# Who sends the finished blocks of the recurrence: SyncE's queue or GpSimd's own

## The chip, the cores and the metric

The kernel runs on one core of a Trainium2 chip. A core has five engines with an instruction stream each: TensorE (PE), VectorE (DVE), ScalarE (ACT), GpSimd (POOL) and SyncE (SP), which here does nothing but issue transfers and wait on semaphores. Transfers (DMAs) run on the core's 16 DMA engines, whichever engine issued them. The metric is the device time of one execution in microseconds (us). The kernel before takes 1922.44 us, the median of three runs (1921.51 to 1926.3).

## The reference, cut to what matters

The input is `x` (2, 64, 256, 256) in float32. There are two layers:

- `x = x + depthwise_conv3x3(ln_c(x))`
- `t = t + rnn(ln_t(t))`, with the 65536 pixels of a batch as a sequence. `Wx = x @ W.T` is normalised over batch and sequence (gamma, beta), and then a scan runs over the sequence: `y = sigmoid(wx_t + y @ V.T)`. The result is called x2 here (x1 is what the convolution left).
- `x = x + linear_attention(ln_c(x))`
- `t = t + expert_ffn(ln_t(t))`: for each of 32 experts the 8 tokens with the highest softmax over the sequence are gathered, pass a two-layer network and are added back.

Only the second of these is touched: the sum `x2 = x1 + y` in the scan and where its blocks go.

## The kernel before, in words

Channels of both batches lie on the 128 partitions, and the 65536 pixels along the free dimension, in 32 blocks of 2048 pixels (`BLOCK`; a block of all partitions is 1 MB in float32). Phases follow each other with a barrier between them: the convolution, a few small instructions for the normalisation, the recurrence (lines 664 to 933), attention with the expert gate, and the gathered expert network.

The scan is made parallel. The sequence is cut into 8 regions (`REGIONS`), each region into 512 chunks of 16 pixels (`CLEN`), and all chunks of a region are advanced together, one pixel a step, after 12 warm-up steps on the pixels before them (`WARM`). So a region takes 28 steps (`STEPS`), and each is done in two groups of 256 chunks (`GROUPS`). One step of one group is a chain over three engines: a matmul by V on PE (line 807), `gain * u + sum` on DVE (line 913, one operand in SBUF, the other and the output in PSUM), and the sigmoid on ACT (line 839), which writes y over the input in the region's buffer `U[r % 4]`. Two regions are in flight at a time, half a region apart (`active(t)`, `HALF` = 14 steps). At the start of the second half of each region DVE also runs `keep_state` (line 884) and `check_states` (lines 893 and 897): a subtraction of two 128x512 SBUF tensors and a maximum. They stand in DVE's program order between steps of the recurrence, so the chain waits while they run.

A region is 4 blocks (`RBLK`). When the y of a region are done (`y_ready`), POOL adds them, block by block, to x1 (line 852, `add_y`), in one of the 4 slots of `xb` (`XSLOTS`), counts `added`, and copies the pixels that attention will use as keys out of the sum (line 655, `take_keys`, which counts `key_taken`). This holds for the first 28 blocks (`LAST` = 28). The last region's x1 is loaded into a free region buffer instead (line 783), POOL adds blocks 1 and 3 of it and DVE blocks 0 and 2 (line 925).

SP's stream sets the order of all transfers of the phase. First it loads regions 0 to 3 (line 748) and the x1 of blocks 0 to 2 (line 756). Then, for each block k from 0 to 27: it waits until the block is added and stores it to the scratch tensor x2 (line 760, `store(k)`), then waits until block k-1 is stored and its keys are taken and loads the x1 of block k+3 into that slot (`load_x1`), and then, for the first 16 blocks, loads block i of region r+4 (line 748, `load_block`; at i = 0 it waits for the check of region r, at i = 3 for the kept state). After block 19 it loads the four x1 blocks of the last region.

POOL issues 12 small DMAs in the first microseconds of the kernel (lines 153 and 155) and indirect ones in the last phase; in the recurrence it issues none.

Of the kernel before, what the change touches and what calls it, by code (L numbers as in the profile page):

```python
# [67 lines left out]
def build_program(nc, x, conv_k, ffn_w, ffn_v, gamma, beta, q_w, q_b, kv_w, kv_b, proj_w, proj_b,  # L68
# [4 lines left out]
    with stack:  # L73
        def sb(name, shape, dt=F32, where=stack):
            return where.enter_context(nc.sbuf_tensor(name, shape, dt))
# [4 lines left out]
        def dram(name, shape, dt=F32):  # L80
            return nc.dram_tensor(name, shape, dt, kind="Internal").ap()
# [6 lines left out]
        x2_d = dram("x2_scratch", (NBLK, P, BLOCK))  # L88
# [44 lines left out]
        with ExitStack() as ph:  # L133
# [7 lines left out]
            @blk.gpsimd  # L141
            def _(pool):
                for t in (w_rows, src["v"], src["q"], src["p"], src["g"], src["kv0"], src["kv1"]):
                    pool.memset(t[:, :], 0.0).then_inc(zeroed, 1)
                pool.memset(eps_c, EPS_C).then_inc(zeroed, 1)
                pool.memset(eps_t, EPS_T).then_inc(zeroed, 1)
                pool.memset(eps_z, EPS_Z).then_inc(zeroed, 1)
                pool.memset(ones[:, :], 1.0).then_inc(zeroed, 1)
                pool.memset(pair_mean[:, :], 0.0).then_inc(zeroed, 1)
                for b in range(B):  # L150
                    d = slice(b * C, (b + 1) * C)
                    for col, vec in ((qb, q_b), (pb, proj_b), (gam, gamma), (bet, beta)):
                        pool.dma_start(col[d, :], vec.rearrange("(c o) -> c o", o=1)).then_inc(vectors_loaded, 16)
                for r in range(4):
                    pool.dma_start(gb[r * E:(r + 1) * E, :], gate_b.rearrange("(c o) -> c o", o=1)).then_inc(vectors_loaded, 16)
# [62 lines left out]
        with ExitStack() as ph:  # L218
            PITCH = W + 2
            XSLOTS = 8  # L220
# [43 lines left out]

            order = sorted((TPB * k + STATS[l], l, k) for l in range(2) for k in range(NBLK))
            round_of = {(l, k): n for n, (_, l, k) in enumerate(order)}

            halos, n = [], 0
# [383 lines left out]
        def take_keys(pool, block, src_rows):  # L652

            v = src_rows.rearrange("p (r w) -> p r w", w=W)
            return pool.tensor_copy(
                xsub[:, bass.ds(block * SUBB, SUBB)].rearrange("p (r w) -> p r w", w=W // SUB),
                v[:, SUB0:ROWS:SUB, SUB0:W:SUB])


        with ExitStack() as ph:  # L660
            XSLOTS = 4
# [9 lines left out]
            xb = sb("x1_block", [P, XSLOTS, BLOCK], F32, ph)  # L671
# [6 lines left out]
            x2_stored = [S(f"x2_stored{j}") for j in range(XSLOTS)]  # L678
            carried, summed, y_ready = S("carried"), S("summed"), S("y_ready")
            fixed, kept, checked = S("fixed"), S("states_kept"), S("checked")  # L680
            added, last_added, key_taken = S("added"), S("last_added"), S("key_taken")
# [17 lines left out]
            def y_done(r, j=GROUPS - 1):  # L699
                return y_no[r, STEPS - 1, j]  # L700

            def state_kept(r):
                return r

            def last_x1(j):

                flat = U[REGIONS % BUFS][:, :, :].rearrange("p n c -> p (n c)")
                return flat[:, j * BLOCK:(j + 1) * BLOCK]
# [17 lines left out]
            def y_in_token_order(r, i):  # L726
                c0 = 1 + i * (BLOCK // CLEN)
                return U[r % BUFS][:, :, c0:c0 + BLOCK // CLEN].rearrange("p n c -> p c n")

            def in_chunks(x):  # L730
                return x.rearrange("p (c n) -> p c n", n=CLEN)
# [12 lines left out]
            @blk.sync  # L744
            def _(sp):
                def load_block(r, i):
                    c0 = 1 + i * (BLOCK // CLEN)
                    sp.dma_start(U[r % BUFS][:, :, c0:c0 + BLOCK // CLEN],
                                 xl_d[r * RBLK + i, :, :].rearrange("p (n c) -> p n c", n=CLEN)).then_inc(region_loaded[r % BUFS][i // GB], 16)

                def load_x1(k):
                    slot = k % XSLOTS
                    if k >= XSLOTS:
                        sp.wait_ge(x2_stored[slot], 16 * (k // XSLOTS))
                        sp.wait_ge(key_taken, k - XSLOTS + 1)
                    sp.dma_start(xb[:, slot, :], x1_d[k, :, :]).then_inc(x1_loaded[slot], 16)

                def store(k):
                    sp.wait_ge(added, k + 1)
                    sp.dma_start(x2_d[k, :, :], xb[:, k % XSLOTS, :]).then_inc(x2_stored[k % XSLOTS], 16)  # L760

                for r in range(BUFS):
                    for i in range(RBLK):
                        load_block(r, i)
                    if r == BUFS - 2:
                        for k in range(XSLOTS - 1):
                            load_x1(k)
                for k in range(LAST):
                    r, i = divmod(k, RBLK)
                    store(k)  # L770
                    if k + XSLOTS - 1 < LAST:
                        load_x1(k + XSLOTS - 1)
                    if r + BUFS < REGIONS:
                        if i == 0:
                            sp.wait_ge(checked, r + 1)
                        if i == RBLK - 1:
                            sp.wait_ge(kept, state_kept(r + 1))
                        load_block(r + BUFS, i)
                    elif r + BUFS == REGIONS and i == RBLK - 1:
                        sp.wait_ge(checked, r + 1)  # L780
                        sp.wait_ge(kept, state_kept(r + 1))
                        for j in range(RBLK):
                            sp.dma_start(last_x1(j), x1_d[LAST + j, :, :]).then_inc(last_x1_loaded, 16)
                n_pool = n_dve = 0
                for j in range(RBLK):
                    if j in POOL_LAST:
                        n_pool += 1
                        sp.wait_ge(added, LAST + n_pool)
                    else:
                        n_dve += 1  # L790
                        sp.wait_ge(last_added, n_dve)
                    sp.dma_start(x2_d[LAST + j, :, :], last_x1(j)).then_inc(last_stored, 16)
                for slot in range(XSLOTS):
                    sp.wait_ge(x2_stored[slot], 16 * len(range(slot, LAST, XSLOTS)))
# [51 lines left out]
            @blk.gpsimd  # L846
            def _(pool):
                pool.memset(U[0][:, :, 0:1], 0.0).then_inc(warm_ready, 1)

                def add_y(r, i, x1_x2):  # L850
                    y = y_in_token_order(r, i)
                    pool.tensor_tensor(in_chunks(x1_x2), in_chunks(x1_x2), y, ALU.add).then_inc(added, 1)  # L852

                for r in range(REGIONS - 1):
                    for i in range(RBLK):
                        k = r * RBLK + i
                        pool.wait_ge(y_ready, y_done(r, i // GB))
                        pool.wait_ge(x1_loaded[k % XSLOTS], 16 * (k // XSLOTS + 1))
                        add_y(r, i, xb[:, k % XSLOTS, :])
                        pool.wait_ge(added, k + 1)  # L860
                        take_keys(pool, k, xb[:, k % XSLOTS, :]).then_inc(key_taken, 1)
                for i in POOL_LAST:
                    pool.wait_ge(y_ready, y_done(REGIONS - 1, i // GB))
                    pool.wait_ge(last_x1_loaded, 16 * RBLK)
                    add_y(REGIONS - 1, i, last_x1(i))
                n_pool = n_dve = 0
                for i in range(RBLK):
                    if i in POOL_LAST:
                        n_pool += 1
                        pool.wait_ge(added, LAST + n_pool)  # L870
                    else:
                        n_dve += 1
                        pool.wait_ge(last_added, n_dve)
                    take_keys(pool, LAST + i, last_x1(i)).then_inc(key_taken, 1)
# [314 lines left out]
        with ExitStack() as ph:  # L1189
# [54 lines left out]

            order = sorted((TPB * k + STATS[l], l, k) for l in range(2) for k in range(NBLK))
            round_of = {(l, k): n for n, (_, l, k) in enumerate(order)}

            def tile_at(t, lag):
# [691 lines left out]
```

## Time and profile before

| | us |
|---|---|
| median of 3 runs (lowest, highest) | 1922.44 (1921.51, 1926.3) |
| the profiled execution, its own time | 1924.74 |
| its span, first to last instruction | 1922.9 |
| PE busy | 1556.5 (81%) |
| DVE busy | 1435.2 (75%) |
| ACT busy | 1238.3 (64%) |
| POOL busy | 1450.8 (75%) |
| recurrence phase, first region load to first load of the next phase | 764.2 to 1074.0 |

The span is one execution as the hardware profiler took it. "Busy" leaves out the issuing of DMAs, semaphores and branches. SPq stands for SyncE's own instructions, here the issuing of transfers, and its duration is how long the issue held SyncE up, not how long the transfer took. In brackets behind an instruction stand the idle time of its engine before it, and what released it; where the engine named there had long been done, a transfer was what was waited for. Windows give, for a stretch, the busy time of each engine, the granted clock of PE as a share of full speed, the busy share of the DMA engines and what they moved.

### The profile page before, as it was taken

To read this page: it belongs to the slowest core of one execution; us is meant where nothing else is said; L and a number is where in the kernel's file an instruction comes from. 1 tells how busy PE (TensorE), PEld (TensorE's weight loads), DVE (VectorE), ACT (ScalarE), POOL (GpSimd) and SP (SyncE) were. 2 spreads that over 40 slices of the span, in tenths; PEclk is the share of its full clock that TensorE was granted. 3 is DMA by queue.
4 is the path that set the end of the run, shared out by engine and by line. 5 is a ranking of instruction groups with operands and counts; after the bars stand their busy time and mean duration, and the time that the engine had idled before them with its cause. 6 is when DMAs were issued, how large, how long until landed. Compare 5 with 4: busy or idle time off the path is not lost. (4 is left out here: it accounts for less than half of the span.)

```text
span 1922.9 us, 24399 instructions
## 1 busy us (share of the span) xinstructions
PE 1556.5 (81%) x5627; PEld 648.4 (34%) x5627; DVE 1435.2 (75%) x2312; ACT 1238.3 (64%) x2178; POOL 1450.8 (75%) x1070
## 2 busy tenths in 40 slices
PE   4899999999999993698886679999999999816100
PEld 1333333333333331365553333333333333206000
DVE  1689999999999985498887547999999999951000
ACT  2777777777777751487875458889888888610000
POOL 2999999999999991058787129999999999901670
PEclk8999999999999996799988779999999999955555
DMA  4578888887888664989996527888888887570111
GB/s 152 163 230 254 251 234 256 251 254 234 253 254 252 192 192 152 313 278 373 368 391 269 219 45 209 287 287 287 285 284 275 278 286 246 192 179 13 2 2 1
DMA packets 114478, 429.81 MB, mean 224 GB/s; under 512 B 46720, under 2 KB 51744, under 8 KB 69280
## 3 DMA queue, kind: packets, MB, share of 16 engines
q1 hardware_dynamic: 92656, 423.78, 69.1%
q10 hardware_dynamic: 18736, 4.29, 1.5%
q8 instruction: 49, 0.80, 0.2%
q0 software_dynamic: 2944, 0.18, 0.1%
q14 instruction: 93, 0.76, 0.1%
HBM read 257.89 MB, written 170.01 MB: 223 GB/s over the span
## 5 line engine op out<-in xcount | busy, mean ns | idle before, releaser
L454 ACT ACTIVATE tap_products<-xn,kk 128x512 f32<-128x512 f32 x384 | 275.0, 718 | 156.6 <-POOL x_and_products L485 149.4
L485 POOL TENSOR_TENSOR x_and_products<-tap_products,x_and_products 128x512 f32<-128x512 f32 x256 | 327.1, 1278 | 41.5 <-POOL x_and_products L485 3.5
L385 PE MATMUL pst<-xn,taps 128*128 128x512 f32 x768 | 351.2, 592 | 0.0
L913 DVE SCALAR_TENSOR_TENSOR pss<-region,bn,pss 128x256 f32<-128x256 f32 x432 | 196.3, 489 | 67.4 <-PE pss L807 64.8
L1495 POOL TENSOR_SCALAR exp_q<-exp_q 128x512 f32<-128x512 f32 x128 | 189.3, 1479 | 73.3 <-ACT exp_q L1446 73.3
L852 POOL TENSOR_TENSOR x_block<-x_block,region 128x2048 f32<-128x2048 f32 x28 | 155.3, 5545 | 110.8 <-ACT region L839 88.5
L543 DVE SCALAR_TENSOR_TENSOR pst<-xn,kk,pst 128x512 f32<-128x512 f32 x256 | 192.2, 751 | 60.4 <-PE pst L385 60.2
L385 PEld LDWEIGHTS pst<-xn,taps 128*128 128x128 f32 x768 | 145.3, 189 | 186.3 <-issue 186.1
L1490 POOL TENSOR_TENSOR sq_norm<-x_ring 128x512 f32<-128x512 f32 x128 | 188.6, 1473 | 5.6 <-DVE x_ring L1542 1.7
L485 POOL TENSOR_TENSOR x_and_products<-tap_products,x_ring 128x512 f32<-128x512 f32 x128 | 163.4, 1277 | 19.2 <-ACT tap_products L454 19.2
L425 ACT ACTIVATE sq<-x_ring 128x512 f32<-128x512 f32 x256 | 157.6, 622 | 16.7 <-POOL x_ring L492 10.1
L1502 POOL TENSOR_TENSOR q_z<-q_map,z_inv 128x512 f32<-128x512 f32 x128 | 163.9, 1281 | 0.0
L492 POOL TENSOR_TENSOR x_ring<-acc,x_and_products 128x512 f32<-128x512 f32 x128 | 163.3, 1276 | 0.0
L807 PE MATMUL pss<-region,vT 128*128 128x256 f32 x480 | 137.5, 411 | 18.4 <-ACT region L839 18.2
L568 DVE TENSOR_TENSOR wx<-psw,rstd_wide 128x512 f32<-128x512 f32 x128 | 137.4, 1073 | 17.1 <-DMA rstd_wide<-rstd_scratch 10.9
L1379 PE MATMUL ps_denominator<-q_map,dT 128*128 128x512 f32 x256 | 138.5, 623 | 9.7 <-DVE q_map L1536 8.4
L1373 PE MATMUL ps_query<-x_ring,qcT 128*128 128x512 f32 x256 | 140.4, 632 | 4.0 <-DVE query L1527 4.0
L394 PE MATMUL psc<-x_ring,cst 128*128 128x512 f32 x256 | 140.1, 630 | 3.4 <-DVE xn L520 3.4
L400 PE MATMUL psw<-x_ring,wcT 128*128 128x512 f32 x256 | 132.9, 603 | 11.6 <-DVE wx L568 11.6
L807 PE MATMUL pss<-warm_state,vT 128*128 128x256 f32 x352 | 108.5, 431 | 40.2 <-ACT warm_state L839 22.1
L839 ACT ACTIVATE region<-pss,bn 128x256 f32<-128x256 f32 x256 | 116.6, 474 | 29.4 <-DVE pss L913 28.7
L1452 ACT ACTIVATE ln_d<-ps_denominator,cols 128x512 f32<-128x512 f32 x128 | 86.8, 678 | 73.2 <-PE ps_denominator L1379 73.0
(246 smaller groups left out, 2954.1 us busy)
## 6 DMA issues: line engine op xcount, KB each, us to landing
rstd_wide<-rstd_scratch SPq DMA_DIRECT2D x128, 512.0 KB, 7.2
x_ring<-in_x SPq DMA_DIRECT2D x32, 1024.0 KB, 5.3
x_scratch<-x_ring SPq DMA_DIRECT2D x32, 1024.0 KB, 4.3
xl_scratch<-wx SPq DMA_DIRECT2D x32, 1024.0 KB, 8.7
region<-xl_scratch SPq DMA_DIRECT2D x32, 1024.0 KB, 11.4
x_ring<-x_scratch SPq DMA_DIRECT2D x32, 1024.0 KB, 5.3
rstd_of_channels<-rstd_scratch SPq DMA_DIRECT2D x64, 512.0 KB, 7.5
out<-x_ring SPq DMA_DIRECT2D x32, 1024.0 KB, 6.6
```

The source lines that it names most:

```text
L385: m = pe.matmul(wide(pst[g % 2]), taps[:, n * P:(n + 1) * P], tap_rows(g, t), start=(n == 0), stop=(n == len(PE_TAPS) - 1))
L425: act.activation(sq[l][:, g % TPB, :], x_tile(g), ACT.Square).then_inc(squared[l], 1)
L454: act.activation(prod[:, n, :, :], tap_rows(g, t), ACT.Copy, scale=kk[:, t:t + 1]).then_inc(products, 1)
L485: pool.tensor_tensor(xr[:, g % XR, :], prod[:, n, :, :].rearrange("p r w -> p (r w)"), xr[:, g % XR, :] if n else x_tile(g), ALU.add).then ...
L492: pool.tensor_tensor(x_tile(g), acc[:, g % 2, :, :].rearrange("p r w -> p (r w)"), xr[:, g % XR, :], ALU.add).then_inc(x1_ready, 1)
L543: dve.scalar_tensor_tensor(out=out, in0=tap_rows(g, t), scalar=kk[:, t:t + 1], in1=wide(pst[g % 2]), op0=ALU.mult, op1=ALU.add).then_inc(a ...
L807: pe.matmul(ps_at(r, j), vT[:, :], before, start=True, stop=True).then_inc(carried, 1)
L852: pool.tensor_tensor(in_chunks(x1_x2), in_chunks(x1_x2), y, ALU.add).then_inc(added, 1)
L913: dve.scalar_tensor_tensor(out=ps_at(r, j), in0=u, scalar=gain_w, in1=ps_at(r, j), op0=ALU.mult, op1=ALU.add).then_inc(summed, 1)
L1490: pool.tensor_tensor(sq[1][:, g % SQSLOTS[1], :], x_tile(g), x_tile(g), ALU.mult).then_inc(squared[1], 1)
L1495: pool.tensor_scalar(e, e, 1.0, None, ALU.min).then_inc(clipped, 1)
L1502: pool.tensor_tensor(qz[:, g % 2, :], qm[:, g % QSLOTS, :], zr[:, g % 2, :], ALU.mult).then_inc(qz_ready, 1)
```

## The change

SP no longer stores the 28 blocks. It still waits for each of them to be added, and its queue then holds only the loads. POOL issues the store itself, behind its own wait for the sum and ahead of the copy of the keys. The store goes out on POOL's own DMA queue. What waits for the stores (`x2_stored`, in `load_x1` and at the end of the phase) is unchanged, and so are the stores of the last region.

```
-                def store(k):
-                    sp.wait_ge(added, k + 1)
-                    sp.dma_start(x2_d[k, :, :], xb[:, k % XSLOTS, :]).then_inc(x2_stored[k % XSLOTS], 16)
-
...
                 for k in range(LAST):
                     r, i = divmod(k, RBLK)
-                    store(k)
+                    sp.wait_ge(added, k + 1)
                     if k + XSLOTS - 1 < LAST:
                         load_x1(k + XSLOTS - 1)
...
                         add_y(r, i, xb[:, k % XSLOTS, :])
                         pool.wait_ge(added, k + 1)
+                        pool.dma_start(x2_d[k, :, :], xb[:, k % XSLOTS, :]).then_inc(x2_stored[k % XSLOTS], 16)
                         take_keys(pool, k, xb[:, k % XSLOTS, :]).then_inc(key_taken, 1)
```

## Rows read from the trace of the kernel before

**Rows 1.** Windows of the recurrence: stretch, its length, busy times, clock, DMA share, GB/s.
```profile
832.00:839.00 7.00, 5.71 (x23) 3.25 (x22) 5.33 (x11) 5.21 (x13) 5.74 (x2) 1.00 0.00 0
900.00:920.00 20.00, 18.19 (x74) 12.83 (x75) 18.22 (x41) 16.99 (x39) 16.54 (x6) 0.91 1.01 374
1000.00:1012.00 12.00, 12.00 (x52) 8.34 (x51) 11.12 (x26) 10.88 (x25) 8.39 (x4) 0.94 1.01 398
1030.00:1046.00 16.00, 13.18 (x35) 5.93 (x33) 7.86 (x17) 7.59 (x16) 15.37 (x6) 0.82 0.56 229
```

**Rows 2.** Timeline of DVE: check_states, regions 1, 4, 5, 6, 7; then line 925.
```profile
867.71 1.77 DVE L893 TENSOR_TENSOR reached<-reached,region 128x512 f32<-128x512 f32 x1
...
958.57 5.22 DVE L893 TENSOR_TENSOR stats<-stats,region 128x512 f32<-128x512 f32 x1
...
993.09 3.22 DVE L893 TENSOR_TENSOR reached<-reached,region 128x512 f32<-128x512 f32 x1
...
1024.73 2.71 DVE L893 TENSOR_TENSOR stats<-stats,region 128x512 f32<-128x512 f32 x1
...
1051.31 5.39 DVE L893 TENSOR_TENSOR reached<-reached,region 128x512 f32<-128x512 f32 x1 [0.54 <-ACT region L839]
...
1057.54 11.99 DVE L925 TENSOR_TENSOR region<-region 128x2048 f32<-128x2048 f32 x2
```

**Rows 3.** Timeline of POOL: start, duration, instruction, [idle before, releaser].
```profile
851.46 5.56 POOL L852 TENSOR_TENSOR x_block<-x_block,region 128x2048 f32<-128x2048 f32 x1
857.09 0.43 POOL L655 COPY xsub<-x_block 128x128 f32<-128x128 f32 x1
863.39 5.54 POOL L852 TENSOR_TENSOR x_block<-x_block,region 128x2048 f32<-128x2048 f32 x1 [5.87 <-ACT region L839]
869.00 0.75 POOL L655 COPY xsub<-x_block 128x128 f32<-128x128 f32 x1
...
957.70 5.54 POOL L852 TENSOR_TENSOR x_block<-x_block,region 128x2048 f32<-128x2048 f32 x1 [2.34 <-DMA x_block<-x_scratch]
...
1015.22 5.55 POOL L852 TENSOR_TENSOR x_block<-x_block,region 128x2048 f32<-128x2048 f32 x1 [6.70 <-DMA x_block<-x_scratch]
...
1050.64 11.45 POOL L852 TENSOR_TENSOR region<-region 128x2048 f32<-128x2048 f32 x2 [5.08 <-ACT region L839]
...
1065.84 4.99 POOL L655 COPY xsub<-region 128x128 f32<-128x128 f32 x4 [3.76 <-DVE region L925]
```

**Rows 4.** Timeline of SP: blocks 9 and 10, then 20 and 21.
```profile
899.27 7.59 SPq L760 DMA_DIRECT2D x_scratch<-x_block  x1
906.96 0.38 SPq L756 DMA_DIRECT2D x_block<-x_scratch  x1
907.38 0.92 SPq L748 DMA_DIRECT2D region<-xl_scratch  x1
908.35 6.74 SPq L760 DMA_DIRECT2D x_scratch<-x_block  x1
...
997.00 0.33 SPq L756 DMA_DIRECT2D x_block<-x_scratch  x1
1002.09 0.34 SPq L760 DMA_DIRECT2D x_scratch<-x_block  x1
```

**Rows 5.** What POOL's own DMA instructions cost elsewhere: direct, then the indirect group.
```profile
2.83 0.57 POOL L153 DMA_DIRECT2D cols<-in_L_conv_proj_b  x1
```

**Rows 6.** Line 1751, all its instructions: durations min/median/max, and idle time before them.
```profile
L1751 POOL DMA_INDIRECT out<-fin,word_of_slot x72: 982/982/1019, 1786.7 to 1878.2; - x72
...
  issue: 21.6, 71
```

**Rows 7.** Region loads (line 748) and first steps (line 830): min/median/max ns, first to last start.
```profile
L748 SPq DMA_DIRECT2D region<-xl_scratch x32: 551/933/9460, 764.2 to 966.3; - x32
...
L830 ACT ACTIVATE warm_state<-region,bn x16: 586/590/600, 774.0 to 992.2; 128x256 f32<-128x256 f32 x16
...
DMA to landing us min/median/max: 6.2/11.4/16.9
```

More of the change, by code:

```diff
@@ L756, in load_x1 @@
                     sp.dma_start(xb[:, slot, :], x1_d[k, :, :]).then_inc(x1_loaded[slot], 16)
-                def store(k):
-                    sp.wait_ge(added, k + 1)
-                    sp.dma_start(x2_d[k, :, :], xb[:, k % XSLOTS, :]).then_inc(x2_stored[k % XSLOTS], 16)
                 for r in range(BUFS):
@@ L769, in _ @@
                     r, i = divmod(k, RBLK)
-                    store(k)
+                    sp.wait_ge(added, k + 1)
                     if k + XSLOTS - 1 < LAST:
@@ L860, in _ @@
                         pool.wait_ge(added, k + 1)
+                        pool.dma_start(x2_d[k, :, :], xb[:, k % XSLOTS, :]).then_inc(x2_stored[k % XSLOTS], 16)
                         take_keys(pool, k, xb[:, k % XSLOTS, :]).then_inc(key_taken, 1)
```

## The prediction

> **What bounds the kernel now.** The page's chain that ended last covers only the last phase, so it says nothing of the recurrence, and the phase has to be read from its own windows. There [rows 1] PE and DVE are busy 18 of 20 us at a granted clock of 0.91, which is the chain matmul, scaled sum, sigmoid; and the DMA engines are full (shares of 1.01 and 1.00 in the two middle rows) from an empty queue at 832 to 839 (0.00) until the share falls to 0.56 after 1030. So two things run side by side: a chain that moves one region each 30.3 us (line 893 from region 1 at 867.71 to region 4 at 958.57, 90.9 for three [rows 2]), and a saturated set of transfers that feeds POOL. I read next what ties them together. The timeline of POOL [rows 3] shows adds of 5.55 us, with POOL idle before some of them, and the timeline of DVE [rows 2] shows the one place where POOL holds the chain up: line 893. It ends 0.55 us after the add of POOL in flight has ended: in region 1 the add ends at 863.39 + 5.54 = 868.93, and line 893 at 867.71 + 1.77 = 869.48; in region 4, 957.70 + 5.54 = 963.24 and 958.57 + 5.22 = 963.79. So a SBUF-to-SBUF subtraction on DVE waits for POOL's add. POOL starts the first add of a region about 4.3 us before line 893 when it is idle, and line 893 then takes the 1.77 of region 1, which stands for four such rows, of regions 0 to 3. Regions 4, 5 and 6 paid 5.22, 3.22 and 2.71: POOL was late, behind loads of x1 (idle 2.34 before 957.70) [rows 3], and met line 893 with a later add. Beyond 1.77 that is 3.45 + 1.45 + 0.94 = 5.84 us in the chain.
>
> The end of the phase is a queue of one: from 1050.64 POOL's two adds, line 893 and DVE's two adds follow each other to 1057.54 + 11.99 = 1069.5 [rows 2, 3], 18.9 us. POOL was idle 5.08 us ahead of it, so it waits for the chain there, not the chain for it.
>
> **SP's side.** SP's 28 stores are held up to 7.59 us each at the issue while the transfers are saturated, against 0.34 when they are not [rows 4]. That looks like the cost to be removed, but SP computes nothing. A block carries three 1 MB transfers there: store 9 is issued at 899.27 and store 10 at 908.35; over 900 to 920 the engines move 374 GB/s, which is 8.4 us for 3 MB, longer than POOL's 6.0 for an add and a copy. SP waits because the DMA engines are full, and the change takes no byte from them. The region loads have slack anyway: the last is issued at 966.3, lands at most 16.9 later, at 983.2, and region 7 begins at 992.2 [rows 7].
>
> **The change part by part.**
>
> Removed: 28 store issues from SP. No engine waits for SP's time itself: worth 0 on the path. What it gives is that a load of x1 or of a region goes to the queue up to 7.6 us sooner, into a queue that is full either way.
>
> Added on POOL: 28 issues, each between the add and the copy. The trace shows no direct 1 MB DMA of POOL. From below the nearest is the direct form on a few bytes, 0.57 [rows 5]; from above the indirect form over 128 rows, 0.98, with 21.6/71 = 0.30 of issue gap behind it, 1.28 [rows 6]. The new one has as many rows as the upper and the form of the lower, and I take 1.0. The far end is that POOL is held at the issue as SP is, up to 7.59; I keep that for a rival. Queued behind the issue on POOL are the copy (0.41) and then the next add, and whoever waits for these: SP's load of x1 through `key_taken`, which has another wait for the store before it anyway, and DVE's line 893. With 1.0 a block costs 7.0 in place of 6.0. In a region that is 28 us of 30.3, so the first three regions keep step with the chain and nothing is lost there.
>
> At the end it counts. From 1015.22 POOL has five adds in a row (blocks 23 to 27), 30.3 us in the trace before (to 1050.64 - 5.08). Five issues add 5.0 and eat the 5.08 of idle time in front of 1050.64: with the upper price of 1.28 the excess is 1.3 us, with the lower none. Cost at 1.0: 0.
>
> Moved: the stores' place among the transfers. Before, all are in one line. The load of block 23's x1 is issued at 997.00 and POOL waits for it until 1015.22, 6.70 us of it idle [rows 3, 4]; store 21 was issued at 1002.09, behind it. If the two queues are served side by side, stores 21 and 22 come ahead of the end of that load, at 1 MB by 398 GB/s = 2.6 us each [rows 1]. So block 23 starts between 0 and 5.2 us later, and from below, if loads issued sooner fill holes, perhaps 1 us sooner. I take +2.5. It passes down the five adds, POOL starts its last two adds at about 1053, and the serial end moves by the same, less what DVE takes in the gap: line 893 and its first add can run while POOL issues and copies (1.4 us per block without a lock on DVE). So +1.5 remains; bounds -1 to +5.2 (with the upper issue price, to +6.5).
>
> Line 893: the waits of regions 4 to 6 will be drawn anew, since POOL's phase shifts by 1 to 4 us there. POOL's add occupies 5.55 of each 7.0 to 8.4 us, and a subtraction that finds it at a random point waits 0.55 to 6.1, by the mean of 3.3 in an add and 0.6 outside, 2.8 over the cycle. Three regions so give about 8.4 against 11.15, a gain of 2.7, but region 3, which now is 1.77, can become late too (+1 by the same mean). Net -1.7, and only as far as POOL isn't last at the end; if POOL's end is what counts, an earlier chain buys nothing. I count -0.5, with bounds of -5.8 (all three aligned) and +7 (four regions at 4 to 5).
>
> On this point the Trainium skill speaks against the change. SBUF — State Buffer, section SBUF: two separate sides, says that a DMA from GpSimd gets its descriptors from GpSimd's own cores and starves while DVE holds the shared ports. Here the row with line 893 at 867.71 shows POOL's copy behind it at 0.75 in place of 0.43 [rows 3], while adds that run beside line 913 stay at 5.54 to 5.56, so the hold is at most one per region. By the page's own example of 620 ns becoming 3100 ns, once in each of eight regions and mostly absorbed, the sum would be higher by an estimated 2.5 us, the last region's.
>
> **The sum.** Against the profiled execution: 0 (SP) + 0 (issues in the idle time) + 1.5 (transfers' order) - 0.5 (line 893) = +1.0, so a span of 1923.9 and a time of 1925.7 for its 1924.74. The profiled execution is 2.3 above the median, so I forecast 1922.44 + 1.0 = 1923.4, own range 1918 to 1929.
>
> **Rivals.**
>
> POOL is last at the end (slower). Place: blocks 23 to 27 and the serial end of 18.9 us. Price: five issues at 1.3 (6.5) plus 5.2 for the later load of block 23, less 5.08 of idle, = 6.6, and up to 9 if each issue is nearer to 1.8. It decides from the point where issue cost times five plus the delay of block 23 passes 5.08 + 5.8 us. For it: all numbers of the trace put POOL within 2 us of the chain. Against: part of the work of DVE slips into POOL's gaps. Time 1929 to 1932; I name 1931. Chance 0.21.
>
> POOL is held at the issue as SP is (slower by much). If the 7 us of [rows 4] come from the DMA engines' side and meet POOL too, a block costs 5.55 + 0.41 + about 5.3 (its own MB at half of 374 GB/s), 11.3; 28 of them are 316 us, against 212 for seven regions at 30.3: about +104, near 2026. For it: SP's row. Against: POOL's indirect ones at 0.98 never wait, though on an idle machine. Chance 0.05.
>
> POOL keeps step (faster). Loads are no longer held behind a store that SP can't get rid of, x1 lands before the region's y is done, regions 4 to 6 go back to 1.77 and the end is not POOL's: -5.8, and line 893 of region 7 may come ahead of POOL's add and save 1 more: 1916. For it: SP's issues of 6.74 and 7.59 [rows 4]. Against: DMA engines without a hole. Chance 0.14.
>
> Two queues raise or lower the rate of the DMA engines. In the trace the rate is 374 with region loads and 398 without them [rows 1]; were the rate of the first the second's, POOL's lateness would vanish and the gain is that of the rival before, which caps it. The Trainium skill (DMA: Bandwidth & Descriptors, issuing engines are not separate DMA queues) says that only issue time is saved; by it this rival is 0 us. I leave its chance in the others'.
>
> **How the numbers follow.** Forecast 0.60, POOL last 0.21, held 0.05, in step 0.14. A measurement of this kernel tells about 0.3%, 5.8 us, from no change. The forecast's range lies almost wholly inside; of the rival in step, nearly all of its 6.4 is just beyond: faster 0.14. Slower is 0.21 + 0.05 and 0.02 of the forecast's edge: 0.28. The range takes the forecast and most of the two near rivals: 1915.5 to 1932.
>
> **What would show it.** POOL's lines get a DMA instruction of about 1.0 us behind each add of line 852; at 0.6 the end stays where it is, at 1.5 POOL's idle time before its last two adds is gone. DMA shares stay at 1.00 with about 374 GB/s, and SP's loads take over the long issues. Add 23 starts at 1015 to 1020. Line 893 of regions 4 to 6 sums to 5 to 14 us. The prediction is wrong if POOL's DMA instructions grow under load, if the saturated stretch ends more than 5 us earlier or later, or if the phases outside 764 to 1074 change.

## The result, and the profile after

The changed kernel takes 1932.26 us (median of 9 runs, 1930.33 to 1939.73), the kernel before 1924.49 beside it (9 runs). The ratio is 1.0044, with a 95% interval of 1.003 to 1.0058: slower by about 8 us. In a second session (e14 below) it was 1931.86 for 1926.27, ratio 1.0028 (1.0015 to 1.0041).

The profiled execution of the changed kernel was the slowest of its nine, so its span (1937.9) overstates the change. The recurrence alone is a better measure. It runs from the first region load to the first load of the next phase: 764.2 to 1074.0 before, 309.8 us, and 768.0 to 1085.7 after, 317.7 us. That is +7.9 us. The second profile of the changed kernel (e14) has 312.2, +2.4; it was the fastest of its twelve executions (1926.35), so the two profiles stand at the two ends of what this kernel does. The phases outside it are 764 to 768 us ahead and 847 to 852 behind in all sixteen profiles of this study, changed or not.

Lines 748, 756 and 655 keep their numbers; what was line 852 (POOL's add) is now 848, line 893 (the subtraction in check_states) is 890, 925 is 922, and the new issue is line 857. First the new line and the x1 loads, each with durations of the issue in ns (min/median/max) and its time to landing:

```profile
L857 POOL DMA_DIRECT2D x_scratch<-x_block x28: 554/565/583, 844.4 to 1057.9; - x28
...
  POOL x_block L848: 8.3, 28
...
DMA to landing us min/median/max: 4.1/9.6/11.8
```
```profile
L756 SPq DMA_DIRECT2D x_block<-x_scratch x28: 327/4582/9014, 807.2 to 1039.8; - x28
...
DMA to landing us min/median/max: 5.6/15.2/19.7
```

An issue costs POOL 0.565 us and the 8.3/28 = 0.30 ahead of it, 0.87 together, the same under a full load as without one. The long issues have moved from SP's stores to SP's x1 loads, up to 9.0 us. The times to landing have to be read with that: they run from the start of the issue, so they contain the time for which the issue held SP. The stores land 9.6 us after the start of their issue (12.1 before), the x1 loads 15.2 us after theirs (8.5 before). From the end of the issue it is the other way round, with medians of 9.0 for the stores (6.1 before) and 8.5 for the x1 loads (8.1 before). The same stretch of the two kernels, from the start of region 2's check to the start of region 3's, with the columns of [rows 1], first before, then after:

```profile
898.01:928.32 30.31, 26.77 (x109) 18.01 (x110) 26.87 (x59) 24.99 (x58) 24.14 (x9) 0.94 1.01 367
```
```profile
901.85:935.31 33.46, 27.86 (x109) 19.09 (x109) 28.72 (x59) 25.01 (x58) 25.28 (x13) 0.90 1.01 375
```

The DMA engines are as full as before (1.01) and move no less, 375 GB/s for 367. What has changed is the chain: for the same 109 matmuls it takes 33.5 us in place of 30.3. The timeline of DVE says why. The check's subtraction of regions 2 and 3, before:

```profile
898.01 1.78 DVE L893 TENSOR_TENSOR stats<-stats,region 128x512 f32<-128x512 f32 x1
...
928.32 1.77 DVE L893 TENSOR_TENSOR reached<-reached,region 128x512 f32<-128x512 f32 x1
```

and after:

```profile
901.85 3.74 DVE L890 TENSOR_TENSOR stats<-stats,region 128x512 f32<-128x512 f32 x1
...
935.31 4.54 DVE L890 TENSOR_TENSOR reached<-reached,region 128x512 f32<-128x512 f32 x1
```

All eight of them, in us, in both profiles of the changed kernel:

| region | 0 | 1 | 2 | 3 | 4 | 5 | 6 | 7 | first seven |
|---|---|---|---|---|---|---|---|---|---|
| before | 1.79 | 1.77 | 1.78 | 1.77 | 5.22 | 3.22 | 2.71 | 5.39 | 18.3 |
| after | 1.77 | 1.77 | 3.74 | 4.54 | 3.52 | 4.16 | 3.02 | 5.66 | 22.5 |
| after, second profile | 1.77 | 1.77 | 1.78 | 4.67 | 3.40 | 3.89 | 2.78 | 5.30 | 20.1 |

Regions 2 and 3 were aligned before: the check met the region's first add near that add's end. In the first profile neither is any longer, in the second only region 3 has lost it. POOL's timeline shows where that comes from. Before, the first wait of an add for x1 is that of block 10:

```profile
907.23 5.55 POOL L852 TENSOR_TENSOR x_block<-x_block,region 128x2048 f32<-128x2048 f32 x1 [1.22 <-DMA x_block<-x_scratch]
```

and after:

```profile
864.81 0.57 POOL L857 DMA_DIRECT2D x_scratch<-x_block  x1 [0.30 <-POOL x_block L848]
...
874.21 5.53 POOL L848 TENSOR_TENSOR x_block<-x_block,region 128x2048 f32<-128x2048 f32 x1 [0.18 <-DMA x_block<-x_scratch]
...
899.50 5.54 POOL L848 TENSOR_TENSOR x_block<-x_block,region 128x2048 f32<-128x2048 f32 x1 [1.49 <-DMA x_block<-x_scratch]
...
1025.03 5.57 POOL L848 TENSOR_TENSOR x_block<-x_block,region 128x2048 f32<-128x2048 f32 x1 [5.09 <-DMA x_block<-x_scratch]
...
1060.59 11.44 POOL L848 TENSOR_TENSOR region<-region 128x2048 f32<-128x2048 f32 x2 [1.67 <-ACT region L835]
...
1075.79 4.99 POOL L655 COPY xsub<-region 128x128 f32<-128x128 f32 x4 [3.76 <-DVE region L922]
```

POOL waits for x1 from block 5 on (874.21; from block 7 in the second profile), where before it was in step until block 10. The first add of region 2 starts at 899.50, 2.35 us ahead of line 890 in place of 4.3, and line 890 ends 0.55 us after it does: 899.50 + 5.54 = 905.04, and 901.85 + 3.74 = 905.59. That is the rule read from [rows 2, 3]. The last two adds start at 1060.59, after 1.67 us of idle time: POOL still waits for the chain there.

How late x1 is can be read for one block in every profile: when it lands, counted from the start of region 0's check. Times of the x1 load of block 8, in us:

| | issue starts | to landing | from first check to landing |
|---|---|---|---|
| before | 880.87 | 8.4 | 51.7 |
| after | 883.61 | 15.8 | 56.5 |
| after, second profile | 878.49 | 14.0 | 55.8 |
| POOL's time alone (e12) | 883.56 | 8.4 | 52.0 |
| small transfers of POOL, stores left with SP (e3) | 883.70 | 8.4 | 52.1 |

It lands 4.1 to 4.8 us later in the changed kernel, and within 0.4 us of before where POOL only loses the time (e12) or issues a small transfer (e3). So it is the real stores' new place that makes x1 late.

One thing more is in the rows around the end. Before, POOL's last copy ends at 1065.84 + 4.99 = 1070.83 and ACT loads the next phase's table at 1071.70; after, they are at 1080.78 and 1083.39:

```profile
1071.70 1.28 ACT L984 ACT_TABLE_LOAD   x1 [20.42 <-PEq L660]
```
```profile
1083.39 1.28 ACT L981 ACT_TABLE_LOAD   x1 [22.43 <-PEq L660]
```

The gap has grown from 0.87 to 2.61 us, and the next phase's first load comes 4.92 us after POOL's last copy in place of 3.18, also 1.74 later.

### The profile page after: what moved, and what is told of

Same layout as the page of the kernel before. It is cut to its first block and busy times, and to the rows that moved or that the text cites. A ratio compares the mean times of both kernels' runs of the same rounds, so it can differ in the third digit from the quotient of the medians.

```text
span 1937.9 us, 24401 instructions
## 1 busy us (share of the span) xinstructions
PE 1558.1 (80%) x5627; PEld 650.3 (34%) x5627; DVE 1439.1 (74%) x2312; ACT 1236.3 (64%) x2178; POOL 1464.9 (76%) x1098
## 5 line engine op out<-in xcount | busy, mean ns | idle before, releaser
L848 POOL TENSOR_TENSOR x_block<-x_block,region 128x2048 f32<-128x2048 f32 x28 | 155.3, 5546 | 100.2 <-ACT region L835 73.3
```

## The experiments

Theories as they are named in the expectations: A, POOL's adds come out of step and meet DVE's subtraction, which stops the chain. B, POOL's added time per block is the cause by itself. D, the chain and POOL's track end close together. E, the gap at the end needs but one DMA of POOL. G, the place of the stores among the transfers puts POOL out of step. The phase is measured in each profile as above; a ratio is to the kernel before on the same chip, with its 95% interval. A profile is of one execution, and some are far from their kernel's median: e12 (1925.35), e10 (1947.66) and e14 (1926.35) are the fastest of theirs, e3 (1932.46) the slowest.

**e1 and e2: no check.** In both kernels the subtraction and the maximum are replaced:

```
-                    dve.tensor_tensor(d, d, U[r % BUFS][:, CLEN - 1, 0:CHUNKS], ALU.subtract).then_inc(dstep, 1)
...
-                    dve.tensor_reduce(dmax[:, r:r + 1], d, AX.X, ALU.max, ...
+                    dve.memset(dmax[:, r:r + 1], 0.0).then_inc(dstep, 1)
```

> The kernel before, with the subtraction and maximum of check_states (lines 893 and 897) left out of all eight regions and a zero written in their place, so the check of the states is left out of the computation. Theory A (the change costs time because POOL's later adds meet DVE's subtraction, which waits for them): this removes the eight waits, 18 us of line 893 and 5 us of line 897 in the chain, and 5 to 6 us at the end; about 1900 us. Theory B (POOL's issues cost the time directly): the same number, the kernel only serves as the base for its partner.

> The changed kernel with the same check left out. Theory A: the difference to the kernel before without its check shrinks from 8 us to that of the barrier at the phase's end, about 2 us, so about 1902 us. Theory B (POOL is simply behind, or the chain is slowed by the transfers): the difference stays at about 8 us, 1908 us.

Measured: 1920.16 (ratio 0.9976, 0.9964 to 0.9988) and 1930.83 (1.0022, 1.0008 to 1.0037). Both expectations of A failed, and for the difference between the two B's 8 us is nearer. Without the check the kernel before gains 6 us and not 24, and the change costs 10.7 us and not 2. The profile of e1 tells why (first DVE's last maximum and its own adds of the last region; then POOL):

```profile
1028.38 0.16 DVE L914 TENSOR_REDUCE dmax<-dmax 128x1 f32<-128x8 f32 x1
1028.46 10.18 DVE L920 TENSOR_TENSOR region<-region 128x2048 f32<-128x2048 f32 x2
```
```profile
1031.03 3.90 POOL L655 COPY xsub<-x_block 128x128 f32<-128x128 f32 x1
1034.90 9.13 POOL L852 TENSOR_TENSOR x_block<-x_block,region 128x2048 f32<-128x2048 f32 x1
...
1050.39 10.99 POOL L852 TENSOR_TENSOR region<-region 128x2048 f32<-128x2048 f32 x2
```

The chain is done at 1028, 262.6 us into the phase, and POOL starts its last adds only at 1050, at 284.6 us. The bound has moved to POOL and the transfers that feed it. Part of the lateness is the early end of the chain itself: DVE's own adds now run beside POOL's, and there a copy takes 3.90 us in place of 0.40 and an add 9.13 in place of 5.52, 7.1 us in all. POOL's track is held in the same way by DVE's adds in e2, e4, e7 and e8. So D holds: in the kernel before, the chain reaches POOL's last adds 286.4 us into the phase and POOL is ready at 281.3; taking away one leaves the other a few us behind. It also shows what the change does to POOL's own track. From e1 to e2 the add of block 23 moves from 247.7 to 255.3 us into the phase (7.6), and the last adds from 284.6 to 295.4 (10.8). A test that frees one of two nearly tied tracks doesn't price the other; the next ones move line 893 without freeing the chain.

**e10: the check one step later.** POOL and all transfers are untouched:

```
                             keep_state(r)
-                            check_states(r - 1)
+                        if s == HALF + 2 and r:
+                            check_states(r - 1)
```

> The kernel before, DVE's check of regions 0 to 6 one step of the recurrence later, POOL and all transfers untouched. In the regions where POOL is in step, the subtraction then starts 6.45 us after the region's first add, at the start of the second, and waits about 5.6 us in place of 1.8. Theory A (what line 893 waits is added to the chain one for one): its first seven sum to 30 to 36 us in place of 18.3, and the phase gets 10 to 17 us longer, 1936 to 1943. Rival F (the wait is hidden, since the two regions in flight overlap it or the transfers bind): under 5 us longer, 1926 to 1931.

Measured: 1948.69, ratio 1.0119 (1.0104 to 1.0134), above A's 1936 to 1943 and far above F's. The first seven subtractions of this kernel run from 5.83 to 5.99 us each, one of them:

```profile
1045.67 5.99 DVE L893 TENSOR_TENSOR stats<-stats,region 128x512 f32<-128x512 f32 x1
```

They sum to 41.2 us, 22.9 more than before, and the phase is 331.1 us, 21.3 more. What line 893 waits is added to the chain almost one for one, as A says, and the sum came out larger than expected because regions 4 to 6 met a start of an add too. Over the profiles where the chain sets the end, the start of POOL's last adds is the start of the first check, plus the seven durations, plus 195 us: before 73.3 + 18.3 + 195 = 286.6 for 286.4; after 74.9 + 22.5 + 195 = 292.4 for 292.6; e13 71.8 + 22.6 + 195 = 289.4 for 290.0; of the other such kernels with the check in its place, six are within 1.1 us of it and e3 is 1.8 us earlier; e10 is within 1.1 too, once its step of 2.2 us is taken off.

**e3: a small transfer for POOL.** SP keeps its stores, POOL issues one of 8 KB per block:

```
                         pool.wait_ge(added, k + 1)
+                        if k:
+                            pool.wait_ge(small_sent, 16 * k)
+                        pool.dma_start(small_d, xb[:, k % XSLOTS, 0:16]).then_inc(small_sent, 16)
```

> The kernel before, SP's stores and their order untouched; POOL in addition issues a small transfer (128 rows of 64 bytes into a scratch tensor) where the change has its store. It has POOL's issue cost and POOL's queue but not the moved bytes. Theory A with the transfers' order as the cause of POOL's lateness: POOL's adds of a block come 6.8 apart where it isn't starved, x1 loads as before, line 893 of the first seven regions stays within 18 to 21 us, and the time is 1924 plus about 2 for the barrier, 1926. Theory B (the 0.87 us per block is the cause): line 893 sums to 22 us or more and the time is 1931 to 1933.

Measured: 1928.57, ratio 1.0016 (1.0005 to 1.0028), between the 1926 of one theory and the 1931 to 1933 of the other. The seven sum to 21.0, the top of A's range, the phase is 313.1 and the gap 2.62. It doesn't separate the theories well: its own wait for the small transfer before left POOL idle for 0.55 to 2.0 us in six blocks, an extra delay that neither theory had. It does show that line 893's sum can rise with x1 on time.

**e12: POOL's time alone.** Two writes of zeros over an unused tensor take the place of the issue:

```
+                        for n in range(2):
+                            pool.memset(taps[:, :], 0.0).then_inc(idled, 1)
+                            pool.wait_ge(idled, 2 * k + n + 1)
```

> The kernel before, with POOL writing zeros over a tensor that is no longer used, twice per block, at the place where the change has its issue: about 0.85 us of POOL's time per block and no DMA of POOL at all. Theory B (POOL's time alone draws line 893 anew): its first seven sum to 21 to 23 us as in the small-issue kernel, phase +3 to +4 us, no extra gap at the end: 1928 to 1930. Theory G (the place of the stores among the transfers is what costs): the sum stays near 18, 1925 to 1927.

Measured: 1928.86, ratio 1.0012 (0.9999 to 1.0024), the two not told apart from no change; by the number it lies in B's range and not in G's. In the profile (blocks 0 and 1)

```profile
835.67 5.54 POOL L853 TENSOR_TENSOR x_block<-x_block,region 128x2048 f32<-128x2048 f32 x1 [68.58 <-ACT region L840]
841.27 0.89 POOL L863 MEMSET taps<- 128x384 f32 x2
...
842.59 5.52 POOL L853 TENSOR_TENSOR x_block<-x_block,region 128x2048 f32<-128x2048 f32 x1
```

a block takes 6.9 us of POOL, no less than in the changed kernel (6.8). Yet the seven subtractions sum to 17.7, regions 2 and 3 stay at 1.77, the phase is 310.0 and the gap 0.85. POOL is idle only 0.96 us ahead of its last two adds. So in this execution the idle time takes up POOL's cost, as the prediction had it, and x1 lands when it did before (the table above): its lateness in the changed kernel comes from the stores' place, as G says. But this is the fastest of twelve executions, 3.5 us below their median, and the timed median leaves room for up to 4.6 us. That POOL's time costs nothing is not shown.

**e4: x1 loads behind the region loads**, in the kernel before:

```
-                    if k + XSLOTS - 1 < LAST:
-                        load_x1(k + XSLOTS - 1)
                     if r + BUFS < REGIONS:
...
                         load_block(r + BUFS, i)
+                    if k + XSLOTS - 1 < LAST:
+                        load_x1(k + XSLOTS - 1)
```

> The kernel before, but SP issues the region load ahead of the load of x1, for the first 16 blocks. Nothing goes to POOL. It makes x1 3.4 us later (1 MB of region at 290 to 340 GB/s), which is about what the moved stores do in the changed kernel. Theory A with the transfers' order: line 893 rises in regions 2 and 3 as in the changed kernel, its first seven sum to 21 to 24 us, and the time is 1928 to 1931 with the barrier as before. Theory B: the order of loads doesn't matter, 1923 to 1925.

Measured: 1943.72, ratio 1.01 (1.0078 to 1.0122), far beyond both expectations. x1 comes so late that POOL's adds are 9 to 10 us apart, and line 893 mostly finds POOL idle: its first seven sum to only 9.1 us. POOL's last adds start 309.1 us into the phase, and POOL ends the phase. The order of the loads matters more than anything else tried here, but through POOL's own track; it is no evidence for A.

**e5 and e6: region loads one block later**, in the kernel before and in the changed one:

```
+                    rl, il = divmod(k - 1, RBLK)
+                    if 0 <= rl < REGIONS - BUFS:
...
+                        load_block(rl + BUFS, il)
```

> The kernel before, each load of a region block issued one block later in SP's order, so that one region load fewer stands ahead of every x1 load. Theory A (x1 comes late behind other transfers, POOL's adds then meet DVE's subtraction): x1 lands some 3 us earlier in the saturated stretch, line 893 of region 4 falls from 5.2 towards 1.8, and the time falls by 2 to 5 us, 1920 to 1923. Theory D (two tracks, the chain and POOL's, end within 5 us of each other and the last x1 loads set POOL's): the same direction, but no more than 4 us. Theory B (POOL's issue cost): says nothing here, 1924.

> The changed kernel with the same shift of the region loads. Theory A and D: the subtraction of regions 2 and 3, 3.7 and 4.5 us in the changed kernel, falls back towards 1.8 and POOL waits less for x1; 1926 to 1929 against the changed kernel's 1932, so a third to two thirds of the loss comes back, and the 1.7 us of the barrier stay. Theory B: 1932, because the issues are untouched.

Measured: 1922.97 (0.999, 0.9979 to 1.0002) and 1931.9 (1.0028, 1.0015 to 1.004). The first isn't told apart from no change, and its region 4 fell to 4.11 and not towards 1.8. The second missed A's 1926 to 1929 and is B's 1932. Line 893's seven sum to 18.0 and 22.0: region 2 of the changed kernel is back at 1.77 and region 3 at 2.90, but regions 4 and 5 rise to 5.07 and 5.17. The x1 of block 8 lands 53.0 us after the first check for 56.5, so an earlier x1 moves the collision and doesn't remove it. It also means that the lateness of one block doesn't set the size of the sum. The phases are 307.7 and 315.2.

**e9, e11, e13 and e14: how many stores.** One small DMA of POOL (e9), then real stores of POOL: 7 (`k % 4 == 0`, e11), 14 (`k % 4 in (0, 2)`, e13) and all 28 once more (e14).

> The kernel before, with one single small transfer (128 rows of 64 bytes) issued by POOL at the start of the recurrence and nothing else changed. Theory E (the phase's end costs 1.7 us more as soon as POOL has issued any DMA in it, however few): POOL's last copy ends 2.6 us ahead of the next phase's first instruction in place of 0.9, phase +1.7 us, time about 1928 for 1926. Rival (the wait at the end is for POOL's many stores to drain): 0.9 us as before.

> Between the two kernels: POOL sends the first block of each of the seven regions, SP the other 21. Theory A with E: 1.7 us at the barrier, and one issue (0.87 us) per region, which POOL's idle time in a region takes up; the line 893 of regions 0 and 1 is at 1.8 as before and the sum of the first seven at 18 to 21 us; 1927 to 1930. Theory B (the cost goes with the number of issues): a quarter of the loss, 1928.

> POOL sends blocks 0 and 2 of each region (14 stores), SP the other 14. What line 893 waits lies between the quarter's 19.8 and the full change's 22.5, time 1928 to 1931. The gap from POOL's last copy to the next phase's table load: 0.9 us if it needs more than 14 DMAs of POOL (rival: grows with their number, 1.8).

> The changed kernel once more, for a second profile of it beside these. If line 893 of the first seven regions again sums to 21 to 24 us and the gap at the end is again 2.6, these two are the change's and not one execution's; the first region's start, 1.6 us later in the first profile, should fall back to 73.3 us after the phase's start. 1932.

| | DMAs of POOL | time, ratio (interval) | line 893, first seven | phase | gap at the end |
|---|---|---|---|---|---|
| before | 0 | 1924.49 | 18.3 | 309.8 | 0.87 |
| e9 | 1 small | 1924.28, 0.9995 (0.9985 to 1.0006) | 17.3 | 306.9 | 0.86 |
| e11 | 7 | 1928.28, 1.0016 (1.0006 to 1.0025) | 19.8 | 312.1 | 0.91 |
| e13 | 14 | 1930.68, 1.002 (1.0004 to 1.0036) | 22.6 | 314.0 | 1.47 |
| e14 | 28 | 1931.86, 1.0028 (1.0015 to 1.0041) | 20.1 | 312.2 | 2.62 |
| after | 28 | 1932.26, 1.0044 (1.003 to 1.0058) | 22.5 | 317.7 | 2.61 |

Line 893's sum splits the profiles: 17.3 to 18.3 in the four with the check and the x1 loads in their place where POOL issues none or one (before, e5, e9, e12), 19.8 to 22.6 in the six where it issues 7 to 28 (e3, e6, e11, e13 and the two of the changed kernel). It doesn't follow the number of stores within these. The x1 of block 8 lands 51.7 us after the first check in e9, 54.5 in e11 and 56.8 in e13, so real stores of POOL delay it there too.

e11 and e13 came out within their expected times; e14's 20.1 is just under the expected 21 to 24.

E is wrong: one or seven DMAs leave the gap alone. It is 1.47 at 14 and 2.61 or 2.62 at 28, with 1 MB and with 8 KB each (e3), and with POOL's last DMA 23 us ahead of it. So it goes with their number, not their bytes and not with a transfer still under way. What is done in it, no row shows, and its cause stays open. The first region's check, 1.6 us late in the first profile of the changed kernel, is at 71.7 in the second, for 73.3 before, so that part was one execution's: no store had been sent by then.

**e7 and e8: relieving both tracks.** The check's subtraction runs on POOL and DVE's maximum two steps later, the region loads come one block later, and the last region's x1 loads after block 23 in place of 19. The check stays in. Of the first edit, POOL's part:

```
+                    pool.wait_ge(y_ready, y_done(r))
...
+                    d = reached[r % 2][:, :]
+                    pool.tensor_tensor(d, d, U[r % BUFS][:, CLEN - 1, 0:CHUNKS], ALU.subtract).then_inc(differed, 1)
                     for i in range(RBLK):
```

> The kernel before with three edits that each relieve one track: the subtraction of the check runs on POOL ahead of a region's first add (DVE keeps the maximum, two steps later), the region loads come one block later, and the last region's four x1 loads come after block 23 in place of block 19. The check stays in the computation. Theory D: the chain loses the 18 us of line 893's first seven, POOL loses the 6 to 8 us that it waits for x1 of block 23 and gains 9 us of subtractions that lie beside the saturated transfers; the phase gets 10 to 15 us shorter, 1910 to 1914. If the transfers as a whole bind: no better than the kernel before without its check, 1918 to 1920.

> The changed kernel with the same three edits. With the collision gone and the x1 of block 23 early, what is left of the change is POOL's issue cost on POOL's track, 0.87 us for each block of the run of adds at the end (5 to 12 of them in a row, 4 to 10 us), and 1.7 us at the barrier. Theory D: 6 to 12 us above its partner. Theory A alone (the collision was all of the loss): 2 us above its partner.

Measured: 1921.06 (0.9976, 0.9965 to 0.9986) and 1924.67 (0.9991, 0.9979 to 1.0004). e7 beats both kernels, but missed D's 1910 to 1914 by 7 us or more and is nearest to the 1918 to 1920 of transfers that bind: the chain is at the last region's check at 270.7 us of the phase, but POOL's adds are still fed at one per 8.4 us through the saturated stretch, and its last two adds start at 285.4. In e8 they start at 290.1, and the next phase's first load comes 4.35 us after POOL's last copy for 2.61. So where POOL's track sets the end, the change costs 4.7 us of it and 1.7 at the gap (phase 306.8 for 300.4), with no check in the chain to collide with. D's 6 to 12 is right in the profile (6.4), but the timed medians are only 3.6 us apart, between D's and the 2 of A.

## Why the prediction was wrong

The forecast was 1923.4, no change; it came out slower by 5.4 to 8.5 us in the two sessions (by the ratios), at 1932.26 and 1931.86, just outside the range and at its edge. Two steps failed: line 893, put at -0.5 and measured at +4.3 and +1.8, and the end of the phase, put at nothing without a term and measured at +1.75. By its own steps:

- **SP's issues are worth nothing.** Right. The held-up issues only changed lines. (The stores at 899.27 and 908.35 are those of blocks 8 and 9 as the kernel counts them.)
- **An issue costs POOL 1.0 us.** 0.87, and it is hidden by POOL's idle time: idle ahead of the last adds went from 5.08 to 1.67, and the profile of e12 shows such a cost with no effect. Right as far as the profiles go; the timed median of e12, 2.6 us above its base, doesn't settle it. Wrong in it is that "the first three regions keep step with the chain": POOL waits for x1 from block 5 or 7 on.
- **Transfers in another order, +1.5.** The shift was there: the add of block 23 starts 257.0 us into the phase for 251.0, and 251.9 in the second profile. Counted from the first check that is 4.4 and 2.5 us later, for a forecast of 2.5 and a bound of 5.2. But it was carried down the wrong path: POOL isn't last at the end, so by that path it costs 0.
- **Line 893 redrawn, -0.5.** This is the step that failed. It measured +4.3 in the first profile and +1.8 in the second (22.5 and 20.1 for 18.3). The step took a random meeting as the new state and credited regions 4 to 6 with it, while the price of losing the aligned regions was put at 1 us for region 3 alone. In the first profile regions 2 and 3 lost 1.96 + 2.77 = 4.7 us, in the second region 3 alone lost 2.9; regions 4 to 6 went from 11.15 to 10.70 and 10.07, so little came back. The transfers' order, priced only at the end, should have been carried to regions 2 and 3: x1 was 4.8 and 4.1 us later already at block 8. None of the signs of being wrong asked for these regions.
- **Missing: the gap at the phase's end, +1.75.** No row of before could show it, since POOL issues no DMA in the recurrence there. It comes with many DMAs of POOL; why, stays open.

Line 893 and the gap make +6.0 of the first profile's +7.9; another 1.6 is the first region's start, and 0.3 is left over. In the second, 1.8 + 1.75 - 1.6 (an early start there) = 2.0 of +2.4. The timed difference of 5.4 to 8.5 us is above the 3.6 and 6.0 of these two, by a part that is within its intervals and that no run here explains. POOL's time is the rival for it: e12 alone was timed 2.6 us above its base, with an interval that holds 0.

Of the rivals, POOL last at the end had the time (1931) but not the mechanism: POOL was still idle before its last adds. It is the mechanism of the same kernel once the check is out of the way (e2, e8). That POOL would be held at the issue is refuted by 554 to 583 ns over all 28. That POOL keeps step went the wrong way: x1 came later, not sooner, although SP no longer issues a store ahead of it.

The prediction's warning from the Trainium skill (SBUF — State Buffer, section SBUF: two separate sides) was that DVE starves GpSimd's DMA. The Trainium skill says it of DVE's instructions in a 2-port mode, and no run here shows that the subtraction is one. The trace shows no starved issue: seven of the 28 overlap the end of line 890, and none of the 28 takes more than 583 ns. The same page of the Trainium skill, section Who interferes with whom, has a nearer rule: a DVE instruction with two SBUF inputs contends with a GpSimd instruction that reads SBUF. The rows agree: line 893 ends 0.55 us after POOL's add in each region where it meets one, and line 913, with one SBUF input, takes 481 to 492 ns in all 432 cases, beside an add or not. The Trainium skill (DMA: Bandwidth & Descriptors, section Queues, rings and completion order) says that each DMA engine takes its queues in turn. No row here shows the turns.

## What to carry to other kernels

Before a store is moved to another queue, ask which loads will now land later, and who works in step with them: with the DMA engines full, the bytes are the same and only the order is new. Price an alignment that the trace shows as an asset that any shift can lose, and carry a shift through every region, not only to the end. Read a time to landing from the end of the issue where the issue itself is held up. When two tracks end within a few us of each other, removing one says nothing about the cost of the other; push a wait up by a known amount (as e10 did) to learn its price.

## What the runs showed that was not expected

- A phase in which POOL issues 28 DMAs ends 1.75 us later after POOL's last instruction than one in which it issues none, one or seven (2.61 or 2.62 for 0.85 to 0.91; 1.47 with 14); where POOL's work outlasts everybody's, it is 2.62 for 0.31, yet the next phase's first load again comes only 1.7 us later (4.35 for 2.61).
- POOL's issue of a 1 MB store takes 0.565 us with the DMA engines full, and an 8 KB one the same 0.56, where SP's issues take up to 7.6 us for a store (before) and 9.0 us for a load (after).
- Line 893 without a collision takes 0.68 us (e4, two regions; 0.69 in e7), so the 1.77 of an aligned region is itself 1.1 us of waiting. Moving it by one step of the recurrence, 2.2 us, made the phase 21.3 us longer (e10).
- DVE's adds hold POOL as POOL's adds hold DVE: where they run side by side, a copy of POOL takes 3.90 us for 0.40 and an add 9.13 for 5.52 (e1).
